# A unit's scores inside the preceding expert stage, and a bias moved to TensorE

## The reference

```python
# x: (4, 512, 128); 16 heads of 8 channels
x = norm(x + rwkv_mix(x));          x = norm(x + x @ W[idx] + b[idx])
x = norm(x + attention(x));         x = norm(x + moe_1(x))     # 8 experts of 176, top 2, and a shared one
x = norm(x + causal_rope_attn(x));  x = norm(x + gqa_and_moe_2(rmsnorm(x)))  # 8 experts of 256, top 2
x = norm(x + causal_gqa_alibi(x))
# last feed-forward, hidden 512, ternary weights w1, w2
x = norm(x + (layer_norm(gelu(layer_norm(x) @ w1.T + b1)) @ w2.T + b2))

# moe_1: h = silu((x @ w1 + b1) * (x @ w3 + b3)), weighted by the gates, then @ w2
# moe_2: h = silu(x @ w1) * (x @ w3), then @ w2, weighted by the gates
# attention: softmax(q @ k.T * scale + mask) @ v, all keys of a block
```

## Time and profile before

| what | us |
|---|---|
| median of 3 runs (1379.30 to 1383.31) | 1381.33 |
| the profiled execution, its own time | 1383.42 |
| its span, first to last instruction | 1381.6 |
| TensorE busy | 1198.1 (87%) |
| VectorE busy | 927.3 (67%) |
| ScalarE busy | 697.0 (50%) |
| GpSimd busy | 269.1 (19%) |
| mean granted TensorE clock, share of full | 0.948 |

### The profile page before, as it was taken

One profiled execution on the slowest core, in us unless ns is written; L12 is line 12 of the kernel. 1 busy time (PEld: TensorE's weight loads), 2 busy tenths in 40 slices (PEclk: granted clock), 3 DMA queues, 4 the chain that ended last, 5 costly groups with the idle time before them and its releaser, 6 DMA issues.

```text
span 1381.6 us, 26337 instructions
## 1 busy us (share of the span) xinstructions
PE 1198.1 (87%) x7977; PEld 634.2 (46%) x8062; DVE 927.3 (67%) x2470; ACT 697.0 (50%) x1268; POOL 269.1 (19%) x560
## 2 busy tenths in 40 slices
PE   3436999999889998899999999999999979989876
PEld 1222223323356655445554555556666534445445
DVE  5867678687465555767778777755555476668676
ACT  2221676776644434556656666663222226666543
POOL 2332211211000012222332332110000211222112
PEclk7565999999999999999999999999999989999988
DMA  8312222310000003313333322100000202221001
GB/s 208 123 51 73 101 59 99 121 35 20 1 1 1 0 1 120 105 53 105 121 94 109 96 77 71 49 3 4 1 1 0 76 12 67 78 77 44 3 0 31
DMA packets 65199, 79.14 MB, mean 57 GB/s; under 512 B 5483, under 2 KB 58068, under 8 KB 64602
## 3 DMA queue, kind: packets, MB, share of 16 engines
q1 hardware_dynamic: 65098, 77.89, 18.0%
HBM read 45.27 MB, written 31.72 MB: 56 GB/s over the span
## 4 chain that ended last, share of the span: by engine, by line
PE 60%; issue 14%; DVE 8%; DMA 6%; ACT 5%; DVEq 3%; POOL 2%; SPq 1%; POOLq 1%; another core or an unknown queue 0%; ACTq 0%
PE bank L1633 11%; PE bank L1618 10%; PE bank L1602 9%; PE bank L1785 6%; PE bank L1786 6%; PE bank L1803 5%; PE bank L1586 3%; DMA KS<-scr_k 3%; PE bank L1620 2%; PE bank L1522 1%; ACT PT L921 1%; DVE M L1198 1%; PE bank L1582 1%; DVE N L1035 1%; PE bank L1516 1%
## 5 line engine op out<-in xcount | busy, mean ns | idle before, releaser
L921 ACT ACTIVATE PT<-bank 128x512 f32<-128x512 f32 (+1 forms) x784 | 425.3, 568 | 257.3 <-PE bank L1620 186.9
L1602 PE MATMUL bank<-KS,QS 125*128 125x512 bf16 (+3 forms) x1024 | 311.2, 332 | 37.1 <-DVE M L1195 13.6
L1198 DVE TENSOR_REDUCE M<-bank 128x1 f32<-128x512 f32 (+2 forms) x400 | 257.5, 684 | 89.3 <-PE bank L1602 53.1
L1195 DVE CUSTOM_DVE_ANT_0 masked_scores<-bank,maskw 128x384 bf16<-128x384 f32 (+1 forms) x384 | 228.6, 622 | 93.7 <-PE bank L1602 85.2
L1618 PE MATMUL bank<-QS,KS 128*128 128x256 bf16 (+1 forms) x953 | 277.4, 320 | 12.3 <-ACT PT L921 8.4
L1633 PE MATMUL bank<-PT,VA 128*32 128x512 f32 (+3 forms) x2048 | 211.6, 485 | 1.3 <-ACT PT L921 1.0
L1618 PEld LDWEIGHTS bank<-QS,KS 128*128 128x128 bf16 x1024 | 99.5, 98 | 222.5 <-ACT PT L921 158.9
L1620 PE MATMUL bank<-identb,maskw 128*128 128x128 bf16 x768 | 148.0, 219 | 12.3 <-issue 6.4
L1602 PEld LDWEIGHTS bank<-KS,QS 125*128 125x128 bf16 x1024 | 100.8, 99 | 115.2 <-DVE M L1198 30.3
L1785 PE MATMUL bank<-XT,MW 128*128 128x512 f32 (+1 forms) x232 | 120.5, 601 | 10.2 <-DVE PT L1375 5.9
L1803 PEld LDWEIGHTS bank<-MW,PT 128*128 128x128 f32 x864 | 110.8, 192 | 40.3 <-issue 37.7
(11 more groups left out here) (229 smaller groups left out, 1453.6 us busy)
## 6 DMA issues: line engine op xcount, KB each, us to landing
scr_q<-PQ SPq DMA_DIRECT2D x48, 384.0 KB, 3.2
QS<-scr_q SPq DMA_DIRECT2D x64, 288.0 KB
scr_k<-PK SPq DMA_DIRECT2D x24, 384.0 KB, 3.7
KS<-scr_k SPq DMA_DIRECT2D x32, 288.0 KB
QS<-MSB SPq DMA_DIRECT2D x192, 4.0 KB
MW<-in_m_w SPq DMA_DIRECT2D x3, 1024.0 KB, 8.2
MW<-in_m_w SPq DMA_DIRECT2D x3, 832.0 KB
scr_k<-PK SPq DMA_DIRECT2D x24, 96.0 KB, 1.9
```

The costliest lines, as they stand in the source:

```text
L921: a.activation(PT[kt % 2][:, js[0]:js[-1] + 1, q0:T], tiles(bank[st_bank(L, g, i)][:, 0:w * len(js)], len(js)), ACT.Exp, scale=c["scale"]) ...
L1195: v.tensor_tensor_reduce(masked_scores[S_ORDER[L][i]][:, 0:kl], bank[S_ORDER[L][i]][:, 0:kl], maskw[:, T - kl:T], -1.0, FLT_MAX, ALU.add, ...
L1198: v.tensor_reduce(M[g % 2][:, t * GH + js[0]:t * GH + js[-1] + 1], tiles(bank[S_ORDER[L][i]][:, 0:kl * len(js)], len(js)), AX_X, ALU.max, ...
L1602: r = mm(s, QS[0:ROWS_SHIFT, g * GH + j, t * P:(t + 1) * P], KS[0:ROWS_SHIFT, kv_slot(L, g, j), 0:kl], start=True, stop=not by_pe)
```

## The change

1. *Early scores.* The first-pass items of unit 0 of block 0 of attentions 1 and 3 move into the last block of the MoE before. `EARLY_S` maps a chunk to an item. They all use bank 7, and so wait for the item before to be reduced. In attention 1, item 10 comes after the MoE's last matmul (`EARLY_N`). At the chain's start only unit 1 is left.
2. *Projections.* The start of a chain is prepared in MoE block 2 (`START_BLOCK = NB - 2`) instead of 3, ScalarE's part for the first MoE one chunk sooner.
3. *Loops written out* for both MoE and all attentions. With constant block numbers the XTS copy falls away. Layer 0 keeps its loops.
4. *Feed-forward bias on TensorE.* The bias is split into three bf16 rows once (`split_up_bias`, GpSimd, in block 0 of the second MoE). A second matmul adds it in PSUM, and Gelu reads PSUM.

```diff
-ACT_START = {L1_MOE: {4: ["v"], 6: ["q0"], 7: ["q1"], 8: ["k0"], 9: ["k1"]}, L2_MOE: {1: ["q"], 2: ["k"], 6: ["q1"], 8: ["k1"]}}
+ACT_START = {L1_MOE: {4: ["v"], 5: ["q0"], 6: ["q1"], 7: ["k0"], 8: ["k1"]}, L2_MOE: {1: ["q"], 2: ["k"], 6: ["q1"], 8: ["k1"]}}
+START_BLOCK = NB - 2
+
+EARLY_S = {1: {2: 0, 3: 1, 4: 2, 6: 3, 7: 4, 8: 5, 9: 6, 10: 7, 11: 8, 12: 9},
+           3: {2: 0, 3: 1, 4: 2, 6: 3, 7: 4, 8: 5, 9: 6, 10: 7, 11: 8, 12: 9, 13: 10}}
+EARLY_N = {1: 10, 3: 11}
...
-        def sequence(L, unit, Fori):
-
-            for g in range(NG):
-                unit(L, 0, g)
-            with Fori(1, NB - 1) as b:
+        def sequence(L, unit):
+
+            for b in range(NB):
                 for g in range(NG):
                     unit(L, b, g)
-            for g in range(NG):
-                unit(L, NB - 1, g)
...
+                    if b == START_BLOCK:
+                        start_pool(AFTER[p])
+                    if is_last(b):
+                        shift(AFTER[p], 0, 0)
+                for b in range(NB):
+                    body(b)
                 post(p, NB - 1)
...
                     for i in range(NT):
-                        act.wait_ge(fb_ready, b * NT + i + 1)
-                        a.activation(HG[b % 2][:, i, :], HG[b % 2][:, i, :], ACT.Gelu).then_inc(fg_ready, 1)
+                        act.wait_ge(fu_ready, b * NT + i + 1)
+                        at_least(act, ft_ready, (b - 1) * 4)
+                        a.activation(HG[b % 2][:, i, :], bank[i][:, :], ACT.Gelu).then_inc(fg_ready, 1)
...
+                    def early(c):
+                        if is_last(b) and c in EARLY_S[AFTER[p]]:
+                            reduce(AFTER[p], 0, 0, EARLY_S[AFTER[p]][c], True)
+
                     for c in range(n):
                         dve.wait_ge(a_evac, k0 + c + 1)
                         if p == L1_MOE:
                             at_least(dve, s1_ready, b * n + c + 1 - back(p, c, 2))
                             v.scalar_tensor_tensor(U1[c % 2], bank[2 + c % 2][:, :], cc("m_b3", c), A1[c % 2], ALU.add, ALU.mult).then_inc(u_ready, 1)
+                            early(c - 1)
...
                             v.tensor_tensor(H1[c % NH1[p]], bank[2 + c % 2][:, :], A1[c % 2], ALU.mult).then_inc(h_ready, 1)
+                            early(c - 1)
...
-            def score(L, b, g, i):
+            def score(L, b, g, i, early=False):
 
                 t, js = S_ITEMS[L][i]
+                to = bank[7] if early else bank[S_ORDER[L][i]]
...
-                at_least(pe, max_done, item(L, b, g, i) + 1 - s_back(L, i))
+                at_least(pe, max_done, item(L, b, g, i) + 1 - (1 if early else s_back(L, i)))
+                if early:
+                    pe.wait_ge(xt_evac, NB * LAYERS[L]["phase"] - (2 if i < 3 else 1))
...
                         elif c == XT_AT:
+                            if b == START_BLOCK:
+                                pe.wait_ge(prep_evac, PREP_BASE[AFTER[p]] + PREP_USES[AFTER[p]])
                             if is_last(b):
-                                pe.wait_ge(prep_evac, PREP_BASE[AFTER[p]] + PREP_USES[AFTER[p]])
+                                pe.wait_ge(max_done, item(AFTER[p], 0, 0, 3))
                             xt(p, b - 1, bank[7])
-                        if is_last(b) and c in PE_START[p]:
+                        if b == START_BLOCK and c in PE_START[p]:
                             prep_pe(AFTER[p], 0, PE_START[p][c])
+                        if is_last(b) and c in EARLY_S[AFTER[p]]:
+                            score(AFTER[p], 0, 0, EARLY_S[AFTER[p]][c], True)
...
-                    at_least(pe, fb_ready, (b - 1) * NT + i + 1)
-                    mm(bank[i][:, :], blk(XT, b)[:, i * P:(i + 1) * P], FW1[:, :], start=True, stop=True).then_inc(fu_ready, 1)
+                    at_least(pe, fg_ready, (b - 1) * NT + i + 1)
+                    mm(bank[i][:, :], blk(XT, b)[:, i * P:(i + 1) * P], FW1[:, :], start=True, stop=False)
+                    mm(bank[i][:, :], pick_parts[:, :], up_bias[:, :], start=False, stop=True).then_inc(fu_ready, 1)
```

102 lines of the change are left out of this document (69 added, 33 removed).

## The result

| | runs | median, us | range, us |
|---|---|---|---|
| before | 4 | 1380.84 | 1379.3 to 1383.31 |
| changed | 4 | 1394.88 | 1391.64 to 1398.99 |

The ratio is 1.0102, 95% interval 1.007 to 1.0133: 14.0 us slower, against +12.1 predicted; 1394.88 us, against 1393.4 predicted with a range of 1385 to 1405. The profiled execution of the changed kernel is the longest of its four, with a span of 1397.2 us and a mean granted clock of 0.947 where the others have 0.953 to 0.958. So the trace lies some 4 us above the median, and stages are compared with that in mind.

What follows compares the result with a forecast made beforehand. TensorE was taken to bound the MoE stages, VectorE's row maxima the transitions. Waits and scores +28.5, transitions -5 and -6.5, loops -1.4, bias -3.5 gave +12.1 on 1381.33: 1393.4 us, range 1385 to 1405.

Steps and rivals of the forecast that it cites:

- The waits: First MoE, last block: TensorE waits nine times for bank 7 to be reduced, 12.6 us; with scores the stage grows 13.8.
- The second MoE: Its last block: ten waits for bank 7, 12.1 us, and 2.6 us of scores, together +14.7 us.
- the chunk-3 wait: Second MoE: the first of ten waits for bank 7, shortened by 0.89 us to 0.4 us.
- rival A: TensorE's clock falls too, as it idles 1.5 us in 4.5 in the MoE blocks: 1412 us, chance 0.12.
- The transitions: From MoE end to the next attention's first transposed scores: early scores save 5 us in the first, 6.5 in the second.
- The projections: MoE blocks 2 and 3: same instructions one block earlier, block 2 grows by what block 3 loses, zero in sum.
- The loops: MoE and attentions: written-out loops drop ScalarE's XTS copy and a wait behind it, -1.4 us (0 to -3).
- the pair of units: First attention: a unit takes 13.17 us inside the loop and 13.16 outside, so looping has no visible cost.
- The bias: Last feed-forward: bias on TensorE frees VectorE and removes two TensorE waits, -3.5 us (0 to -6).
- B: Early scores in the MoE: the waits are short, only the scores' 4.8 us remain, 1369 us; chance 0.07.
- C: Whole kernel: savings larger, each bound at its far end with waits of +24, 1381.8 us; chance 0.08.
- D: First MoE: the stack lands late, the early pass starts after chunk 2, waits up to 3 us, 1396 us; chance 0.08.

Runs made afterwards that it cites:

- e1_no_early: The changed kernel with unit 0's first scores and maxima back at the chain's start, everything else kept: 1368.92 us, 0.993 of the kernel before.
- e2_same_chunk: The changed kernel with each early item's maximum moved behind H of its own chunk, still one bank: 1368.55 us, 0.9916 of the kernel before.
- e4_loops_only: The kernel before with the MoE and attention loops written out alone, on all engines: 1374.65 us, 0.9968 of the kernel before.
- e7_gates_signal: e2_same_chunk with TensorE's first transposes of the late gates waiting for the gates alone, not their parts: 1365.29 us, 0.9902 of the kernel before.
- e11: The kernel before with both the feed-forward bias on TensorE and the loops written out: 1370.58 us, 0.9932 of the kernel before.
- e9: The kernel before with the loops over blocks written out on VectorE alone: 1376.55 us, 0.997 of the kernel before.
- e10: The kernel before with the loops written out on all engines but VectorE: 1375.96 us, 0.9965 of the kernel before.
- e3_bias_only: The kernel before with the feed-forward bias on TensorE alone: 1375.53 us, 0.9967 of the kernel before.

## Why the prediction was right

**The total** was nearer than its parts, and that is luck. The sum had +17.0 us for the early pass (28.5 - 5 - 6.5) and -4.9 for the rest. Measured are some +24 for the early pass (1.0102 against 0.993) and -10 for the rest (e1_no_early). Errors of 7 and 5 us with opposite signs left +14.0 against +12.1.

**The waits** were right in place, cause and nearly in number. In the first MoE nine of them sum to 10.3 us in the trace of the changed kernel, against 12.6. Each was 0.29 us shorter than drawn. VectorE starts the maximum 0.08 us before U's row ends and the score follows it by 0.06 rather than 0.10; the other 0.16 is the different start of the idle time, 1.05 us after the first down matmul in the profile and 0.89 in the sum. Counted as in the sum, the nine make 11.8 us. That the stage grew by 14.0 where 13.8 were predicted is in part luck. e2_same_chunk takes 10.6 of it away; what it has over e1_no_early, the scores less what they fill of a wait at the block's end, is 1.7 (2.2 - 1.0 predicted); and 1.7 more is in e1_no_early and e4_loops_only too, which is the fall of the clock at 411 us, a thing the sum had at nothing.

**The second MoE** was under-sized: +18.9 against +14.7. Here the failed step is the chunk-3 wait, "0.4", taken as an ordinary wait shortened by two down steps. It was 3.27 us, for VectorE's sum and statistics stand ahead of that maximum. The nine others were 0.93 to 1.13 against 1.2 to 1.35. All ten make 12.7 us against 12.1. With 0.16 us more for each, as above, they are 14.3. The 16.6 us that e2_same_chunk removes are these less the one of 1.06 that it keeps, the clock behind the long wait, and a second fall in block 2, where the projections now are:

```profile
1040.15 1.08 PE L1621 MATMUL bank<-WC,XT 128*128 128x32 f32 x8 [1.82 <-ACT KF L912]
1041.06 1.33 PE L1837 MATMUL bank<-XT,MW 128*128 128x512 f32 x2
1042.18 1.91 PE L1838 MATMUL bank<-XT,MW 128*128 128x512 f32 x2
```

That second fall isn't the change's own: e1_no_early and e2_same_chunk have the same projections there and no fall.

**The clock** (rival A) neither fell for good nor stayed. The six waits in a row of 1.15 to 1.28 us at the end of the first MoE went by at full clock (a mean of 1.00 from 504.90 to 558.65 us); behind the 3.27 us the two up pairs ran at the lower level, and the last block of the second MoE had a mean clock of 0.97 (1084.00 to 1141.56 us). So one of the prediction's own signs of being wrong, a clock under 1 in these blocks, came true in the second MoE, at a small price. The many waits in a row did not bring the fall that A expected of them. A's reading that gaps up to 1.75 us went by at full clock was wrong in its upper end: the eight transposes behind the 1.75 us took 1.97 us, and from 1328.80 to 1339.00 us the granted clock was 0.50. That gap lay in a stretch that was already at the lower level; the longest in the first MoE that went by at full clock was 1.53 us, before 413.15.

**The transitions** gave 3.9 and 6.0 us, against 5 and 6.5. The norm at 565.62 waited 2.23 us for the root, as written. What the first fell short by is in part the clock: 0.66 there, and the items that follow the norm take 0.42 and 0.31 us where they take 0.27 and 0.22 at the full one. e2_same_chunk and e7_gates_signal have the same code at this place and took 14.9 us at a mean of 0.77 and 15.5 at 0.67. The rest of the 1.1 us is open.

**The projections**, zero, fit the measurement (e11 against e1), which can't tell them from 3 us.

**The loops** were mis-sized: -1.4 predicted with a bound of 3, -4.5 measured (1.8 to 7.2). The step that failed is the pair of units: the 13.16 and 13.17 us were of the first attention, whose units have no masked maximum that TensorE waits for. In attention 1 of the kernel before VectorE stood 0.30 us in front of such maxima:

```profile
641.41 0.69 DVE L1195 CUSTOM_DVE_ANT_0 masked_scores<-bank,maskw 128x512 bf16<-128x512 f32 x1 [0.30 <-issue]
```

and TensorE then waited 1.17 us for them, and not 0.79 as with VectorE's loops written out. The Trainium skill's remark in "Runtime: NRT & Kernel Launch", section "Instruction fetch mechanics", that a taken branch outside the fetched window stalls, points to a gain. No run here shows the fetch itself. The trace also shows a stand of 0.42 us in straight code that the loop didn't have, and e9 and e10 leave open where the gain is.

**The bias** was right: -3.6 by e3_bias_only, and the last stretch fell by 4.4 us in its trace. In the changed kernel TensorE's waits there are

```profile
1352.29 1.88 PE L1926 MATMUL bank<-ident,PT 128*128 128x128 f32 x8 [0.43 <-ACT PT L1028]
...
1381.72 1.09 PE L1926 MATMUL bank<-ident,MW 128*128 128x128 f32 x8 [1.34 <-DVE MW L1514]
```

where it had 1.75 and 2.50 us: they shrank and did not vanish as written. The clock of that stretch is 0.97, against 0.88 (and 0.97 in e3_bias_only too).

**"By that no layout with a single bank can avoid the wait"** was wrong, and it is the most useful error here. The Trainium skill in "PSUM — Partial Sum Buffer", section "PSUM bank collisions raise a hardware error", asks that a bank be guarded by semaphores, so that it isn't written while it is read; from that follows that a second write waits for the read, not that the read must be late. In e2_same_chunk eighteen of the nineteen waits are gone with one bank. The sum took VectorE's place for the reduce as given and was right on the change as it stood. It would have misled anyone who mended it.

**The rivals.** B (the waits are short) would have needed the reduce ahead of TensorE's next score, which is what e2_same_chunk does, and that gave 1368.55 where B gave 1369. Its mechanism was not in this change, and the near number is partly luck: B's sum has -7.7 for the early pass, which brought nothing measurable, and -4.9 for loops and bias, which measured -8 to -10. Of C's savings only that of the loops passed its far end (-3, against -4.5), and the larger waits hid it. D did not happen: item 0 at 512.95 us had no wait.

## What to carry to other kernels

When a small step is slipped into another stage's pipeline, count for each engine not only its cost but what it waits for there: a maximum reduced one step later than it could be made TensorE idle for 1.2 us on average, nineteen times, and moving the same instruction half a chunk up in VectorE's order was worth 26 us. Look for the odd chunk: the longest wait stood where the neighbour block's statistics are done. And price the benefit by itself before mending the cost: with the waits gone, the early pass was worth nothing that these runs could tell, since of the 10 us that it saves in two transitions the MoEs take half back.
